# A four-layer graph network on one core: one-hots written as bf16 and weighted into fp32 by ScalarE, a different order inside a tick of the first layer, and normalizing moved from VectorE to ScalarE

## The reference, cut to what matters

```python
x = _layernorm(x + gat(x, edge_index, ...))          # layer 0
x = _layernorm(x + schnet(x, edge_attr_128, ...))    # layer 1
x = _layernorm(x + gcn(x, edge_index, W, b))         # layer 2
x = _layernorm(x + gin(x, edge_index, ...))          # layer 3

def _layernorm(x): m = mean(x); v = var(x); return (x - m) / sqrt(v + 1e-5)
# gat:    h = x @ W; e = leaky_relu(a_s[src] + a_d[dst]); e = exp(e - segment_max(e));
#         out = segment_sum(h[src] * e / segment_sum(e)) + bias      (with self loops)
# schnet: f = ssp(edge @ We1 + be1) @ We2 + be2; agg = segment_sum((x @ Wn)[dst] * f, src);
#         x + ssp(agg @ W2 + b2) @ W3 + b3,  ssp(v) = softplus(v) - log 2
# gcn:    segment_sum((x @ W.T)[src] / sqrt(deg[src] * deg[dst])) + b (with self loops)
# gin:    relu((segment_sum(x[src]) + x) @ W1 + b1) @ W2 + b2
```

## Time and profile before

| | |
|---|---|
| median of three runs | 5311.9 us |
| the profiled execution, its own time | 5312.49 us |
| its span in the trace | 5310.7 us |
| busy: POOL / DVE / PE / ACT | 3524.7 / 2760.1 / 2721.2 / 1319.8 us |
| longest group: matmuls of the plain layers, L1498 | 1277.1 us |
| gathers of the four layers, L1572 | 856.3, 803.9 and 1593.0 us |

### The profile page before, as it was taken

One profiled execution on the slowest core, in us unless ns is written; L12 is line 12 of the kernel. 1 busy time (PEld: TensorE's weight loads), 2 busy tenths in 40 slices (PEclk: granted clock), 3 DMA queues, 4 the chain that ended last, 5 costly groups with the idle time before them and its releaser, 6 DMA issues. The chain is left out here.

```text
span 5310.7 us, 54159 instructions
## 1 busy us (share of the span) xinstructions
PE 2721.2 (51%) x13301; PEld 2238.2 (42%) x13381; DVE 2760.1 (52%) x7383; ACT 1319.8 (25%) x3951; POOL 3524.7 (66%) x3833
## 2 busy tenths in 40 slices
PE   1477767777588864443333644434443244444445
PEld 1356555556466653333333433333333133333333
DVE  2699888888788863333333533333333533333334
ACT  4587666667366630000000200000000000000001
POOL 0677666767255557777777467777777377777773
PEclk8798898989677765555555655555555555555556
DMA  4666666667376742221111122212223222222224
GB/s 75 175 168 166 150 155 157 161 155 172 33 227 221 230 151 53 53 53 51 52 51 50 40 61 53 52 50 53 53 53 51 52 53 52 51 52 52 53 53 50
DMA packets 430927, 489.97 MB, mean 92 GB/s; under 512 B 86459, under 2 KB 333071, under 8 KB 430614
## 3 DMA queue, kind: packets, MB, share of 16 engines
q0 software_dynamic: 131904, 288.49, 23.2%
q1 hardware_dynamic: 295828, 197.27, 13.4%
q10 hardware_dynamic: 2882, 0.70, 0.1%
HBM read 359.63 MB, written 126.50 MB: 92 GB/s over the span
## 5 line engine op out<-in xcount | busy, mean ns | idle before, releaser
L1498 PE MATMUL bank<-arena 128*128 128x128 f32 x4992 | 1277.1, 438 | 1968.8 <-DVE arena L884 1690.8
L1572 POOL DMA_INDIRECT arena<-node_table,pick x1664 | 1593.0, 957 | 650.7 <-issue 507.2
L1498 PEld LDWEIGHTS bank<-arena 128*128 128x128 f32 x4992 | 1111.4, 328 | 2134.3 <-DVE arena L884 1863.8
L872 DVE TENSOR_TENSOR acc<-acc,bank 128x128 f32 x2496 | 719.1, 288 | 2101.7 <-PE bank L1498 1810.5
L1572 POOL DMA_INDIRECT arena<-gat_table,pick x832 | 856.3, 1029 | 348.2 <-issue 237.4
L1572 POOL DMA_INDIRECT arena<-message_table,pick x832 | 803.9, 966 | 255.8 <-issue 253.3
L1179 ACT COPY xt<-bank 128x512 f32<-128x512 f32 (+1 forms) x39 | 21.6, 554 | 2131.8 <-PE bank L1438 2131.7
L884 DVE TENSOR_TENSOR arena<-iota_free,local 128x512 f32<-128x512 f32 x624 | 428.0, 686 | 3.4 <-issue 2.4
L1487 PE MATMUL bank<-arena 128*128 x1664 | 338.4, 367 | 46.9 <-DVE arena L898 40.7
L1487 PEld LDWEIGHTS bank<-arena 128*128 128x128 f32 x1664 | 290.2, 263 | 114.2 <-issue 114.2
L763 DVE SCALAR_TENSOR_TENSOR acc<-acc,arena,bank 128x129 f32 x832 | 287.4, 345 | 66.0 <-DVE acc L763 34.1
(11 more groups left out here) (219 smaller groups left out, 3373.2 us busy)
## 6 DMA issues: line engine op xcount, KB each, us to landing
message_table<-arena POOLq DMA_DIRECT2D x208, 256.0 KB, 3.3
filter_table<-arena SPq DMA_DIRECT2D x196, 256.0 KB
arena<-filter_table SPq DMA_DIRECT2D x624, 64.0 KB
xt<-edge_cols SPq DMA_DIRECT2D x131, 256.0 KB
arena<-local_rows SPq DMA_DIRECT2D x208, 128.0 KB
arena<-node_table,pick POOLq DMA_INDIRECT x1664
arena<-edge_cols SPq DMA_DIRECT2D x65, 256.0 KB
arena<-gat_table,pick POOLq DMA_INDIRECT x832
```

The lines of the kernel that those rows point to most:

```text
L872: e.tensor_tensor(a, a, bank[6 + t % 2][:, s * P:(s + 1) * P], ALU.add).then_inc(sums, 1)
L1498: ins = e.matmul(bank[6 + n % 2][:, s * P:(s + 1) * P], hot[n % 2][:, s, :], gathered[:, slot(n, s), 0:D], start=True, stop=True)
L1572: e.indirect_dma_start(out=dst, out_offset=None, in_=table, in_offset=bass.IndirectOffsetOnAxis(ap=index, axis=0)).then_inc(done, 16)
```

## The change

1. **One-hots of the first layer.** `iota_half` and `local_half`, bf16 copies of `iota_free` and `local[0]`, are made once by two casts. `gat_hot` compares these and writes bf16 into two new buffers `flags`. `gat_weigh` reads `flags` and writes the weighted fp32 one-hots into `hot`, which has two buffers in place of three. So `gat_hot` now waits for `hot_weighted`, and `gat_weigh` for `product_done`.
2. **Order in a tick.** On ACT the tick opens with `f_made_of` and `f_soft`; `gat_dst`, `gat_weight`, `gat_weigh` follow, and the background is last. On DVE `f_plus_of` is woven in as a piece that skips round 1, so that it stands after the second of the four `gat_sum` additions.
3. **Norm stages.** ACT normalizes, with four `activation(Identity)` instructions per set that take two pointers each, the scale `rstd` and the bias `shift`. DVE makes `shift` = -mean x rstd in one small instruction per set. Lags behind it grow by one tick in norm stages 1 and 2.
4. **Bias rows.** The bias of the layer is added to `x_sb` by DVE during the plain layer before it (`add_row`, every eighth tick, 13 per layer): half of `out_row` in plain layer 1 (`half_row`, since the stage takes 2 x), `L2_gnn_b` in layer 2, `L3_gnn_b2` in layer 3. In return norm stage 3 loses the addition L973, and norm stages 2 and 4 lose the matmul L1444. Norm stage 1 keeps its L850.
5. `table_out` is one semaphore in place of two, and three constant rows live in the ring `gathered` until it is used.

```diff
@@ gat_hot, on DVE
-                if t > 2:
-                    e.wait_ge(product_done, t - 2)
-                e.tensor_tensor(hot[t % 3][:, :, :], iota_free[:, :].unsqueeze(1).to_broadcast([P, GRP, P]),
-                                local[0][:, i:i + GRP].unsqueeze(2).to_broadcast([P, GRP, P]),
+                if t > 1:
+                    e.wait_ge(hot_weighted, t - 1)
+                e.tensor_tensor(flags[t % 2][:, :, :], iota_half[:, :].unsqueeze(1).to_broadcast([P, GRP, P]),
+                                local_half[:, i:i + GRP].unsqueeze(2).to_broadcast([P, GRP, P]),
                                 ALU.is_equal).then_inc(hot_made, 1)
@@ f_plus_of and the loop of DVE
             def f_plus_of(u):
+                yield
                 e.wait_ge(f_log, u + 1)
...
+                if 0 <= t - 3 < FTICKS:
+                    pieces.append(f_plus_of(t - 3))
                 weave(pieces, background, background_turns(t))
-                if 0 <= t - 3 < FTICKS:
-                    run(f_plus_of(t - 3))
@@ gat_weigh, on ACT
+                if t > 1:
+                    e.wait_ge(product_done, t - 1)
                 for s in range(GRP):
-                    ins = e.activation(hot[t % 3][:, s, :], hot[t % 3][:, s, :], ACT.Copy, scale=weight[:, s:s + 1])
+                    ins = e.activation(hot[t % 2][:, s, :], flags[t % 2][:, s, :], ACT.Copy, scale=weight[:, s:s + 1])
@@ the loop of ACT
             for t in range(TICKS + 13):
-                weave([], background, background_turns(t))
+                for lag, fn in ((5, f_made_of), (3, f_soft)):
+                    if 0 <= t - lag < FTICKS:
+                        fn(t - lag)
                 for lag, fn in ((4, gat_dst), (9, gat_weight)):
                     if (t - lag) % GT == 0 and 0 <= t - lag < TICKS:
                         fn((t - lag) // GT)
-                for lag, fn in ((5, f_made_of), (10, gat_weigh), (3, f_soft)):
-                    if 0 <= t - lag < (TICKS if fn is gat_weigh else FTICKS):
-                        fn(t - lag)
+                if 0 <= t - 10 < TICKS:
+                    gat_weigh(t - 10)
+                weave([], background, background_turns(t))
@@ before the loop, on DVE
+            own(e.tensor_copy(iota_half[:, :], iota_free[:, :]))
+            t = own(e.tensor_copy(local_half[:, :], local[0][:, :]))
+            after(t)
@@ norm stages: DVE makes the shift, ACT normalizes
-            def normed(n, rs, x):
+            def shift_of(n, rs):
+                b0, b1 = span(n)
                 e.wait_ge(rs, n + 1)
-                for k, b in enumerate(SETS[n]):
-                    ins = e.tensor_scalar(x_sb[:, b, :], res[n % 4][:, k, :], moments[:, b, 0:1], rstd[:, b:b + 1],
-                                          ALU.subtract, ALU.mult)
-                ins.then_inc(x, 1)
+                e.scalar_tensor_tensor(shift[:, b0:b1], moments[:, b0:b1, 0], -1.0, rstd[:, b0:b1], ALU.mult, ALU.mult
+                                       ).then_inc(shifted, 1)
...
+            def normed(n, stage, x):
+                e.wait_ge(shifted, stage * NS + n + 1)
+                for k, b in enumerate(SETS[n]):
+                    ins = e.activation(x_sb[:, b, :], res[n % 4][:, k, :], ACT.Identity, scale=rstd[:, b:b + 1],
+                                       bias=shift[:, b:b + 1])
+                ins.then_inc(x, 1)
@@ the bias rows: DVE in the plain layers, no longer DVE or PE in the norm stages
+            def add_row(n, row):
+                b0, b1 = span(n)
+                return own(e.tensor_tensor(x_sb[:, b0:b1, :], x_sb[:, b0:b1, :],
+                                           row[:, :].unsqueeze(1).to_broadcast([P, b1 - b0, D]), ALU.add))
...
-            def plain_layer(which, base):
+            def plain_layer(which, base, row):
                 for t in range(TICKS + 4):
+                    if t % 8 == 4 and t // 8 < NS:
+                        added = add_row(t // 8, row)
...
-                    q = own(e.tensor_tensor(xb[n % 2][:, 0:b1 - b0, :], x_sb[:, b0:b1, :],
-                                            rows["L2_gnn_b"][:, :].unsqueeze(1).to_broadcast([P, b1 - b0, D]),
-                                            ALU.add))
-                    after(q)
...
-                    times(n, bank[4], nplus, mats["L1_gnn_W3"], n2_second, out_row)
+                    times(n, bank[4], nplus, mats["L1_gnn_W3"], n2_second)
...
-                    times(n, bank[4], nplus, mats["L3_gnn_W2"], n4_second, rows["L3_gnn_b2"])
+                    times(n, bank[4], nplus, mats["L3_gnn_W2"], n4_second)
```

More of the change, by code:

```diff
@@ L251, in build_program @@
         gathered = part([P, RING, D + 2])
-        hot = [part([P, GRP, P]) for _ in range(3)]
+        hot = [part([P, GRP, P]) for _ in range(2)]
+        flags = [part([P, GRP * P], BF16).rearrange("p (s n) -> p s n", s=GRP) for _ in range(2)]
         pad_col = part([P, 1])
+        rows.update({name: gathered[:, 6 + k, 0:D] for k, name in enumerate(ROWS[:3])})
         gat_w, att_prod = gathered[:, 4, :], gathered[:, 5, 0:D]
@@ L580, in vector @@
             e.tensor_tensor(filter_row[:, :], bank[4][:, 0:P], rows["L1_gnn_be2"][:, :], ALU.add)
-            e.tensor_tensor(out_row[:, :], bank[4][:, P:2 * P], rows["L1_gnn_b3"][:, :], ALU.add
-                            ).then_inc(fold_taken, 1)
+            q = own(e.tensor_tensor(out_row[:, :], bank[4][:, P:2 * P], rows["L1_gnn_b3"][:, :], ALU.add))
+            after(q)
+            e.tensor_scalar(half_row[:, :], out_row[:, :], 0.5, None, ALU.mult).then_inc(fold_taken, 1)
             e.wait_ge(keys_made, 1)
@@ L887, in plain_layer @@
                 e.wait_ge(plain_summed, base + STEPS)
+                after(added)
             e.memset(degree_part[:, STEPS:SW], 0.0)
@@ L920, in vector @@
             e.wait_ge(acc_zeroed, NS + 1)
-            plain_layer(1, 0)
-            for t in range(NS + 12):
-                n = t - 11
+            plain_layer(1, 0, half_row)
+            for t in range(NS + 13):
+                n = t - 12
                 if 0 <= n < NS:
@@ L984, in vector @@
             e.wait_ge(n3_acc, NS)
[L985 removed]
+            e.wait_ge(table_out, 2 * 16 * NS)
+            plain_layer(0, 2 * STEPS, rows["L3_gnn_b2"])
             for t in range(NS + 8):
@@ L1179, in keep @@
                 e.copy(buf[n % 2][:, 0:width(n)], bk[:, 0:width(n)]).then_inc(kept, 1)
-            for t in range(NS + 8):
-                n = t - 7
+            for t in range(NS + 9):
+                n = t - 8
                 if 0 <= n < NS:
@@ L1515, in tensor @@
             e.wait_ge(plain_summed, STEPS)
-            for t in range(NS + 12):
-                n = t - 10
+            for t in range(NS + 13):
+                n = t - 11
                 if 0 <= n < NS:
```

71 lines of the change are left out of this document (40 added, 31 removed).

## The result

The changed kernel takes 5233.69 us (median of 4 runs, 5227.17 to 5252.95) against 5308.18 us of the kernel before on the same chip (4 runs): ratio of the means 0.9866, 95% interval 0.9838 to 0.9894, so the gain is 1.3% and clear of the spread. Forecast were 5262 us and a range of 5205 to 5293. The profiled execution took 5235.59 us.

The account below looks back on a forecast made before the run. DVE was taken to pace the loop above POOL's floor, DVE to bound norm stages 1 and 3, PE 2 and 4. From 5312.5 us, -28 - 7 - 14.5 + 1 - 5 + 3 = -50.5 gave 5262 us, range 5205 to 5293.

Parts of the forecast that it names:

- What bounds the loop: First-layer loop: DVE sets the pace above POOL's floor, so the loop can shrink by at most 97.4 us.
- One-hots: First-layer loop: bf16 comparison stays at 0.689 us because one source repeats each place 128 times; weighing stays at 0.392 us.
- The filter's instruction among the additions, -19: Loop on DVE: L769 between two additions saves 0.24 us in odd ticks, 23.5 us, less a fifth: 19 us.
- Rival C: Loop: softplus comes late, L769 waits 0.3 us in each of 196 ticks, 59 us lost; 5350 us, chance 0.08.
- Turns, -10: Loop, 14 turns of the sort: early softplus gains 1 us where no edge weights are due; 10 us in all.
- PE's new stop: Turns of the sort: PE stuck between the halves until ACT's late copy; over 4 us each would refute the prediction.
- Loop, -28: First-layer loop: filter's instruction 19 and turns 10 make 29 us less; two casts before it cost 1 us.
- Norm stages, -25.5: Four norm stages, normalizing moved to ACT: -7, +1, -14.5 and -5 us for stages 1 to 4.
- Added rows, +3: Plain layers: 39 added DVE instructions, half holding a gather's start 0.15 us on average: +3 us, bounds 0 and 23.

Follow-up runs that it names:

- thin pair: Kernel before and changed kernel, both with half of the loop's gathers left out from the 15th tick on: 5277.08 and 5210.77 us.
- thin kernels: Half of the loop's gathers left out: kernel before 5277.08 us, changed 5210.77, before with only the filter's instruction woven in 5267.57, with only ACT's order 5283.66.
- thin before: Kernel before with two of four gathers left out in each loop tick from the 15th on: 5277.08 us.
- thin weave: Kernel before with half of the loop's gathers left out and the filter's instruction woven in after the second addition, ACT's order old: 5267.57 us.
- thin changed kernel: Changed kernel with half of the loop's gathers left out from the 15th tick on: 5210.77 us.

## Why the prediction was right, point by point

The forecast was 5262 us and the measured 5233.69 lies inside its range. The mechanism holds for the norm stages and for what bounds the loop. Two terms were mis-sized or missed, both in the same direction, and one of them by chance.

- **What bounds the loop.** Right: POOL's waits were the room to gain, and 59.3 of 97.4 us were used.
- **One-hots.** Right at 0.686 us (forecast 0.689), and for the reason given. Weighing from bf16 costs 0.387 us, the same.
- **The filter's instruction among the additions, -19.** The step was right, the size too small: outside the turns the ticks of the first two profiles lost 28.6 us. The gap itself came out at 0.25 us in column 0 of the table and 0.39 in column 2, where 0.24 was forecast. Column 3, the ticks with logits, gained 0.19 us that the forecast left at nothing. But the term was priced as independent of ACT's order, and it is not: alone it brings 10.7 us. The prediction's sum has no term for what each edit gives the other, so that the two terms together came near the measured value is in part luck. Rival C was close to it: the filter's instruction moved early does wait for the softplus, but because of the edge weights in front of it, and only with ACT's old order.
- **Turns, -10.** The ticks at the turns took 8.5 us less in the first two profiles and 8.9 in the thin pair (325.2 to 316.3). The wait changed its place as forecast, and PE's new stop took 44.0 us over 14 turns, 3.1 each, under the 4 that would have refuted it. But the size is right only in the pair: in the thin kernels the waits for softplus and mask in these ticks fell by 5.7 us, and most of the rest is busy time that the weave saves there as elsewhere. As a price for the order alone it was wrong: that costs 12.1 us at the turns.
- **Loop, -28.** Mis-sized by the filter's term: -35.9 between the gathers (the 28.6 and 8.5 us above are counted between one-hots, and so sum to a little more). POOL's waits were expected at about 70 us and came out at 38.1.
- **Norm stages, -25.5.** Right: -27.5 in the sum, stage by stage within 1.7 us, and the same on a second chip. The two-pointer activation takes 0.484 us (forecast 0.474). That ACT now sets norm stage 2 shows in the waits too: from 2946 us to the stage's end ACT waits for 2.5 us in all, and DVE waits for its softplus (L973 <- ACT L1158) 19.5 us, where it was 11.7.
- **Added rows, +3.** The cost of the rows themselves had the right sign and was small: 8 gathers that start during an added row take over 1.0 us, and all that start there are 1.5 us longer in sum. The stages around them missed sign and cause. The plain layers gave 7.7 us, the messages 4.3, and no instruction was taken from either. Two kernels with the same code in plain layer 1, thin before and thin weave, differ there by 6.4 us, and so does the gathers' busy time. The groups of that layer in the two:

```profile
L1576 POOL DMA_INDIRECT arena<-message_table,pick x832 | 787.3, 946 | 255.8 <-issue 253.3 <-DMA message_table<-arena 2.5
```

```profile
L1577 POOL DMA_INDIRECT arena<-message_table,pick x832 | 793.8, 954 | 255.7 <-issue 253.2 <-DMA message_table<-arena 2.5
```

It is the meeting of the earlier trace rows: 60, 35 and 37 gathers take over 1.0 us in the three plain layers before, 26, 32 and 52 in the changed kernel. What all gathers of a layer take over 0.944 us sums to 19.2, 11.5 and 12.2 us before and 7.7, 10.3 and 17.2 in the changed kernel. The differences, -11.5, -1.2 and +5.0, are those of the layers' lengths to 0.1 us. That the number of such meetings is a matter of phase is concluded from the spread among kernels with the same code there, 8 to 60 in plain layer 1, and was not tested by itself. As far as the runs show, these 7.7 us are luck and no gain of any part of the change. Where the messages' 4.3 us come from was not tried; their length in thin kernels with the same code there spans 487.3 to 494.7 us too.

So the median came out 28.3 us below the forecast: 8 in the loop, 15 in plain layers and messages, 2 in the norm stages, 2 before the first gather, and 2 between the profiled execution and the median.

## What to carry to other kernels

Before adding up two edits of order, ask of each what stands in front of the instruction it makes urgent: here moving a consumer earlier paid in full only once its producer no longer stood behind a wait for the consumer's own engine. So price the pair, and try each alone. A gain on an engine that feeds a gather-bound stage is worth what the gathers leave, and that differs between chips: here 74 us on one and 43 on another. Where stages with unchanged code move by some us, look for a phase effect (here which gathers happen to start during a two-source instruction) before naming a cause.

## What the runs showed of the hardware

- A bf16 comparison of two tensor sources, 128x512: 0.687 us with each element of one source repeated 128 times, 0.420 with the same row as both sources and no repetition.
- A gather that starts while DVE runs an instruction with two sources in SBUF is mostly lengthened, to 1.42 us from 0.94 in the earlier trace rows: 132 of 152 such gathers took over 1.0 us in the kernel before, and none of the 995 that started during an addition with one source in SBUF and one in PSUM. With one-source one-hots the means are 950 and 949 ns in place of 972 and 968, on the same chip. The thin changed kernel has 2 gathers over 1.0 us in plain layer 1 and 60 in layer 2.
- On three chips the queue of the gathers stood still again and again: in the eight kernels traced there between 20 and 26 times in 700 us of plain layer 1 (from 100 us behind its first gather), for 4.0 to 4.5 us on average. A plain layer took 138 to 160 us more, and the kernel before 11 to 12% more. In the first two profiles and the thin kernels no pause over 1.5 us occurs there.
